# Linear attention in a decoder layer: paired feature tiles, 64-row fp32 scores by row halves, scores copied by ScalarE, later keys cleared by GpSimd, and GpSimd's sums behind the rows of norm 2

## The reference

```python
h = _ln(x, g1, beta1)
q = _phi((h @ wq).reshape(b, s, H, DH), proj)     # _phi(x) = elu(x @ proj) + 1
k = _phi((h @ wk).reshape(b, s, H, DH), proj)
v = (h @ wv).reshape(b, s, H, DH)
def step(carry, qkv_t):                            # scan over the tokens, so causal
    kv = kv + k_t[..., :, None] * v_t[..., None, :]
    ksum = ksum + k_t
    num = jnp.einsum('bhd,bhde->bhe', q_t, kv)
    den = jnp.einsum('bhd,bhd->bh', q_t, ksum) + 1e-06
    return ((kv, ksum), num / den[..., None])
x = x + attn.reshape(b, s, H * DH) @ wo
h2 = _ln(x, g2, beta2)
x = x + (gelu(h2 @ w1 + b1) @ w2 + b2)
```

## Time and profile before

| what | value |
|---|---|
| device time, median of 3 runs | 2541.67 us (2539.79 to 2542.41) |
| the profiled execution | 2538.4 us, of which the span from first to last instruction is 2536.7 us |
| mean granted TensorE clock | 0.949 of full speed |
| busy: PE, PEld | 2320.6 us (91%), 1752.5 us (69%) |
| busy: DVE, ACT, POOL | 1872.8 us (74%), 1573.8 us (62%), 678.4 us (27%) |

### The profile page before, as it was taken

How to read it: one execution, slowest core, us unless ns; L and a number is a source line. 1 busy time by engine, 2 the same in 40 slices (tenths; PEclk the granted TensorE clock), 3 DMA queues, 4 the chain that set the end, 5 groups by cost and what they waited for, 6 DMA issues and landing times. The chain is left out here.

```text
span 2536.7 us, 61265 instructions
## 1 busy us (share of the span) xinstructions
PE 2320.6 (91%) x20194; PEld 1752.5 (69%) x20194; DVE 1872.8 (74%) x4914; ACT 1573.8 (62%) x3456; POOL 678.4 (27%) x1179
## 2 busy tenths in 40 slices
PE   5998988988987589999999999999999999879997
PEld 3866856857757357676667767776767667667886
DVE  5667557657665478888888888888888888666657
ACT  4344244253351278888888888888888888544444
POOL 2001001001001234444444344444444444200003
PEclk8999999999999799999999999999999999758999
DMA  4100000000000200000000000000000000023302
GB/s 124 37 1 1 0 0 0 0 0 0 0 0 1 90 11 10 15 14 8 13 8 13 8 13 8 13 8 13 11 11 13 8 7 1 1 68 100 100 1 59
DMA packets 45652, 50.08 MB, mean 20 GB/s; under 512 B 19120, under 2 KB 37664, under 8 KB 45504
## 3 DMA queue, kind: packets, MB, share of 16 engines
q1 hardware_dynamic: 45504, 48.45, 6.6%
HBM read 44.78 MB, written 3.67 MB: 19 GB/s over the span
## 5 line engine op out<-in xcount | busy, mean ns | idle before, releaser
L1393 POOL TENSOR_SCALAR p_norm<-p,p_rec 112x375 f32<-112x375 f32 x512 | 305.1, 596 | 728.4 <-DVE p_rec L1235 674.7
L1117 ACT ACTIVATE p<-s_neg,neg_max 112x375 f32<-112x375 f32 x512 | 311.3, 608 | 131.6 <-DVE neg_max L1230 101.3
L1239 DVE TENSOR_TENSOR pt_lo<-b_t,pt_hi 125x336 f16<-125x336 f32 x512 | 259.5, 507 | 115.7 <-ACT pt_hi L1123 100.1
L1008 PE MATMUL b_t<-ident,p_norm 112*125 112x112 f32 x1536 | 287.7, 297 | 9.5 <-POOL p_norm L1393 8.9
L1215 DVE SCALAR_TENSOR_TENSOR k<-b_pb,k 64x375 f16<-64x375 f32 x512 | 280.9, 549 | 13.5 <-ACT k L1108 2.5
L1230 DVE CUSTOM_DVE_ANT_0 s_neg<-b_s,mask_bias 112x375 f32<-112x375 f32 x512 | 275.9, 539 | 0.8 <-PE b_s L1002 0.7
L1108 ACT ACTIVATE k<-b_pb 64x375 f16<-64x375 f32 x512 | 243.9, 476 | 26.7 <-PE b_pb L64 23.7
L1008 PEld LDWEIGHTS b_t<-ident,p_norm 112*125 112x125 f32 x1536 | 217.0, 193 | 54.3 <-POOL p_norm L1393 31.5
L1123 ACT ACTIVATE pt_hi<-b_t 125x336 f16<-125x336 f32 x512 | 226.5, 442 | 34.2 <-issue 16.1
L417 ACT ACTIVATE o_hi<-a_pb 128x448 f16<-128x448 f32 x64 | 34.9, 545 | 320.3 <-PE a_pb L309 320.1
L638 POOL TENSOR_SCALAR a_rstd<-a_mom 112x4 f32<-112x4 f32 x24 | 5.5, 230 | 769.3 <-DVE a_mom L470 769.3
(11 more groups left out here) (247 smaller groups left out, 6871.2 us busy)
## 6 DMA issues: line engine op xcount, KB each, us to landing
w_raw<-in_L_ffn_W_dram SPq DMA_DIRECT2D x16, 1024.0 KB, 7.5
ctx<-in_ctx_dram SPq DMA_DIRECT2D x32, 375.0 KB
out_dram<-c_z SPq DMA_DIRECT2D x8, 448.0 KB, 3.2
x_sb<-in_x_dram SPq DMA_DIRECT2D x1, 3136.0 KB, 19.4
ff<-in_L_attn_w_dram SPq DMA_DIRECT2D x2, 1024.0 KB, 7.0
b_stage<-in_L_xattn_Wkv_dram SPq DMA_DIRECT2D x2, 1024.0 KB, 10.3
mask<-in_mask_BxS_bf_dram SPq DMA_DIRECT2D x32, 41.0 KB, 2.6
a_raw<-in_L_attn_wq_dram SPq DMA_DIRECT2D x1, 1024.0 KB, 5.0
```

Of the source, the lines that this page charges most:

```text
L1008: mm = pe.transpose(t_ps[h % 2][0:JP, t * T:(t + 1) * T], p_norm[:, h % 4, t * JP:(t + 1) * JP], ident[0:T, 0:T])
L1117: act.activation(p32[:, h % 4, :], s_neg[:, h % 2, :], ACT.Exp, bias=neg_max[:, h % 4:h % 4 + 1], scale=-1.0, accum_out=p_sum[:, h % 4:h % ...
L1239: dve.tensor_tensor(pt_lo[:, h % 4, :], t_ps[h % 2][0:JP, 0:JT * T], pt_hi[:, h % 4, :], ALU.subtract).then_inc(pt_lo_done, 1)
L1393: pool.tensor_scalar(p_norm[:, h % 4, :], p32[:, h % 4, :], p_rec[:, h % 4:h % 4 + 1], 0.0, ALU.mult, ALU.add).then_inc(p_norm_done, 1)
```

## The change

The k features get paired tiles like q's: `kt` has 8 tiles of 128 partitions, written by one DVE instruction per tile; `kz` and its memset are gone. A score product reads 64 partitions of `kt` and `qt`: heads with even number the partitions 0 to 63, heads with odd number 64 to 127. Units are renumbered so that an even unit holds four even heads and the next one their four neighbours; `scores` is issued for two units at even steps, the two halves in turn, each half into its own PSUM bank. It waits for `s_copied` of both units before. ACT copies each unit's scores to `sm` (`take_scores`), which has four buffers where it had two, and POOL clears the later keys there in place with a select (`mask`). DVE's `mask` and the matrix `causal` are gone. `turn_output` is issued at odd steps with four transposes. POOL's two sums wait for `rows_done[1]` too, the rows of norm 2.

```diff
@@ -114,18 +113,18 @@
...
-        NSM = 2
+        NSM = 4
...
-        kz = sb("kz", [P, H, GT], F32)
+        kt = sb("kt", [P, KI, GT], F32)
...
-        o32 = sb("o32", [T, 4, 4 * DH], F32)
+        o32 = sb("o32", [T, 2, 8 * DH], F32)
...
@@ -146,6 +145,12 @@
+        def unit(u):
+            b, quad = divmod(u, 4)
+            first = 8 * (quad // 2) + quad % 2
+            return b, [first + 2 * i for i in range(4)]
...
@@ -164,7 +169,7 @@
...
-                if TURN_AT <= t < UNITS + TURN_AT and (t - TURN_AT) % 2 == 0:
+                if TURN_AT <= t < UNITS + TURN_AT and (t - TURN_AT) % 2 == 1:
...
@@ -284,31 +289,33 @@
...
-                b, quad = divmod(u, 4)
-                at_least(pe, s_masked, UNITS * g + u - 1)
-                for i in range(4):
-                    h = 4 * quad + i
-                    mm = pe.matmul(s_ps[u % 2][0:T, i * T:(i + 1) * T], kz[:, h, b * T:(b + 1) * T],
-                                   qt[:, h // 2, b * T:(b + 1) * T], start=True, stop=True)
-                mm.then_inc(s_ready, 1)
+                b, heads = unit(u)
+                cols = slice(b * T, (b + 1) * T)
+                at_least(pe, s_copied, UNITS * g + u)
+                for i, h in enumerate(heads):
+                    for r in range(2):
+                        rows = slice(DH * r, DH * (r + 1))
+                        mm = pe.matmul(s_ps[r][0:T, i * T:(i + 1) * T], kt[rows, h // 2, cols], qt[rows, h // 2, cols],
+                                       start=True, stop=True)
+                        if i == 3:
+                            mm.then_inc(s_ready, 1)
...
-                b, quad = divmod(u, 4)
+                b, heads = unit(u)
...
-                for i in range(4):
+                for i, h in enumerate(heads):
...
-                                   v1[0:T + 1, b, 4 * quad + i, :], start=True, stop=True)
+                                   v1[0:T + 1, b, h, :], start=True, stop=True)
...
-            def turn_output(g, u):
-                pe.wait_ge(o_done, UNITS * g + u + 1)
-                ps = claim(use(g, "O", u // 2)) if u % 2 == 0 else bank(use(g, "O", u // 2))
-                for m in range(2):
-                    c = (2 * (u % 2) + m) * T
-                    mm = pe.transpose(ps[:, c:c + T], o32[:, u % 4, m * P:(m + 1) * P], ident[0:T, 0:T])
-                if u % 2 == 1:
-                    mm.then_inc(pb_ready, 1)
+            def turn_output(g, j):
+                pe.wait_ge(o_done, UNITS * g + 2 * j + 2)
+                ps = claim(use(g, "O", j))
+                for m in range(4):
+                    mm = pe.transpose(ps[:, m * T:(m + 1) * T], o32[:, j % 2, m * P:(m + 1) * P], ident[0:T, 0:T])
+                mm.then_inc(pb_ready, 1)
...
@@ -320,12 +327,12 @@
...
-                    if t < UNITS:
+                    if t < UNITS and t % 2 == 0:
...
-                    if TURN_AT <= t < UNITS + TURN_AT:
-                        turn_output(g, t - TURN_AT)
+                    if TURN_AT <= t < UNITS + TURN_AT and (t - TURN_AT) % 2 == 1:
+                        turn_output(g, (t - TURN_AT) // 2)
...
@@ -417,12 +424,20 @@
...
+            def take_scores(g, u):
+                act.wait_ge(s_ready, UNITS * g + u - u % 2 + 2)
+                at_least(act, av_done, UNITS * g + u + 1 - NSM)
+                act.activation(sm[0:T, u % NSM, :], s_ps[u % 2][0:T, 0:4 * T], ACT.Identity).then_inc(s_copied, 1)
...
+                    if t < UNITS and t % 2 == 0:
+                        take_scores(g, t)
+                        take_scores(g, t + 1)
...
@@ -489,21 +504,9 @@
...
-                if kind == "K":
-                    for r in range(2):
-                        rows = slice(DH * r, DH * (r + 1))
-                        ins = dve.scalar_tensor_tensor(kz[rows, 2 * i + r, :], ps[rows, 0:GT], 0.0, phi_exp[rows, i % 2, :],
-                                                       ALU.max, ALU.add)
-                else:
-                    ins = dve.scalar_tensor_tensor(qt[:, i, :], ps[:, 0:GT], 0.0, phi_exp[:, i % 2, :], ALU.max, ALU.add)
-                ins.then_inc(free_of(u), 1)
-            def mask(g, u):
-                dve.wait_ge(s_ready, UNITS * g + u + 1)
-                at_least(dve, av_done, UNITS * g + u + 1 - NSM)
-                dve.tensor_tensor(sm[0:T, u % NSM, :].rearrange("p (i t) -> p i t", t=T),
-                                  s_ps[u % 2][0:T, 0:4 * T].rearrange("p (i t) -> p i t", t=T),
-                                  causal[:, :].unsqueeze(1).to_broadcast([T, 4, T]), ALU.mult).then_inc(s_masked, 1)
+                dst = kt if kind == "K" else qt
+                dve.scalar_tensor_tensor(dst[:, i, :], ps[:, 0:GT], 0.0, phi_exp[:, i % 2, :], ALU.max,
+                                         ALU.add).then_inc(free_of(u), 1)
...
@@ -514,7 +517,8 @@
...
-                dve.tensor_tensor(o32[:, u % 4, :].rearrange("p (i d) -> p i d", d=DH), ps[:, :, 0:DH],
+                dst = o32[:, u // 2 % 2, :].rearrange("p (i r d) -> p r i d", r=2, d=DH)[:, u % 2, :, :]
+                dve.tensor_tensor(dst, ps[:, :, 0:DH],
...
@@ -540,8 +544,6 @@
...
-                    if t < UNITS:
-                        mask(g, t)
...
@@ -616,7 +618,6 @@
...
-            dve.wait_ge(kz_zeroed, 1)
...
@@ -639,21 +640,28 @@
...
+            def mask(g, u):
+                settle(pool, passed, (s_copied, UNITS * g + u + 1))
+                rows = sm[0:T, u % NSM, :].rearrange("p (i t) -> p i t", t=T)
+                pool.affine_select(out=rows, in_=rows, compare_op=ALU.is_ge, fill=0.0, base=0, pattern=[[0, 4], [1, T]],
+                                   channel_multiplier=-1).then_inc(s_masked, 1)
...
+                    if t < UNITS:
+                        mask(g, t)
...
-                at_least(pool, rows_done[2], g)
+                settle(pool, passed, (rows_done[1], g + 1), (rows_done[2], g))
...
-            pool.memset(kz[:, :, :], 0.0).then_inc(kz_zeroed, 1)
...
@@ -699,17 +707,14 @@
...
-            pool.memset(causal[:, :], 1.0).then_inc(consts_done, 1)
...
-            pool.wait_ge(consts_done, 3)
+            pool.wait_ge(consts_done, 2)
...
-            pool.affine_select(out=causal[:, :], in_=causal[:, :], compare_op=ALU.is_ge, fill=0.0, base=0,
-                               pattern=[[1, T]], channel_multiplier=-1).then_inc(consts_done, 1)
...
-            pe.wait_ge(consts_done, 5)
+            pe.wait_ge(consts_done, 3)
...
```

More of the change, by code:

```diff
@@ L106, in layer1 @@
         b2 = sb("a_b2", [T, D], F32)
-        causal = sb("causal", [T, T], F32)
-        load_layer1(nc, a, x_sb, ident, half_neg, consts_done, causal, hi, lo, (g1, be1, g2, be2, b1, b2), sb_in, psum_in, sem)
+        load_layer1(nc, a, x_sb, ident, half_neg, consts_done, hi, lo, (g1, be1, g2, be2, b1, b2), sb_in, psum_in, sem)
         def pair(name, k, c0, n, width):
@@ L220, in layer1 @@
         h_hi_done = [sem(f"a_h_hi_done{i}") for i in range(2)]
-        kz_zeroed, pads_done = sem("a_kz_zeroed"), sem("a_pads_done")
+        pads_done = sem("a_pads_done")
         relu_done, exp_done = sem("a_relu_done"), sem("a_exp_done")
-        s_ready, s_masked, av_done, rec_done, o_done, o_hi_done = (
-            sem(f"a_{n}") for n in ("s_ready", "s_masked", "av_done", "rec_done", "o_done", "o_hi_done"))
+        s_ready, s_copied, s_masked, av_done, rec_done, o_done, o_hi_done = (
+            sem(f"a_{n}") for n in ("s_ready", "s_copied", "s_masked", "av_done", "rec_done", "o_done", "o_hi_done"))
         xs1_done, xs_done = sem("a_xs1_done"), sem("a_xs_done")
@@ L661, in _, with load_layer1 @@
             ln_rstd(NG - 1, 2)
-def load_layer1(nc, a, x_sb, ident, half_neg, consts_done, causal, hi, lo, vectors, sb_in, psum_in, sem):
+def load_layer1(nc, a, x_sb, ident, half_neg, consts_done, hi, lo, vectors, sb_in, psum_in, sem):
     stack = ExitStack()
```

## The result

The changed kernel takes 2421.74 us (median of 4 runs, 2419.57 to 2433.45) against 2540.73 us for the kernel before, run again beside it: ratio 0.9544, interval 0.9511 to 0.9577. The profiled execution has a span of 2420.4 us, 116.3 less than before.

A forecast was written before the change was run, and what follows sets the result against it. TensorE was taken to bound the attention and feed-forward stages, waits the projection stage. Terms 5.2 + 1.2 + 50.4 + 4.1 + 17.6 = 78.5 us off 2538.4 gave 2459.9, stated as 2462 us; range 2440 to 2514.

The forecast's parts named there:

- Sum: Whole kernel: start 5.2, prologue K tiles 1.2, projection stages 50.4, group 7's rows 4.1, attention stages 17.6; 78.5 us saved.
- Start: Kernel start: kz's memset goes, sm's doubles, PE starts 5.2 us earlier; prologue K tiles save another 1.2 us.
- Norm 2 and K tiles: Projection stage: first wait 3.9, clock 1.8, K tiles' pace 0.9, shorter kz wait 0.6; 7.2 us per group.
- Rival B: Projection stage gives back half as ACT's work comes to the front: 3.9 instead of 7.2 us, 2485 us; chance 0.09.
- Scores: Attention stage: row halves overlap, a pair takes 1.17 us with switches instead of 1.57; 3.2 us saved per group.
- Rival A: Attention-stage scores: row halves don't overlap, a pair costs 1.95 us, 50 us more than forecast, 2512 us; chance 0.20.
- Attention stage: Each of 8 groups: scores save 3.2 us, uncovered first copies cost 1.0; 2.2 us net, 17.6 in all.
- Last group: Group 7: norm 2's rows in front of T2 save 4.1 us; its attention stage saves 2.2.
- Select: POOL's masking select of 448 columns in the attention stage takes 0.7 us, covered in steady state.
- C: Attention stage: POOL's selects hold up DVE's line 477 rows through the port, 45 us, 2507 us; chance 0.06.
- D: Attention stage: POOL's select is slow, at 2.3 us it loses 98 us, 2560 us, slower than before; chance 0.04.
- the 0.31 us wait: Attention-stage group start: the only part of DVE's masks the prediction took to be on PE's path.

The follow-up runs named there:

- b_act100: Kernel before plus 100 empty ScalarE instructions at the start of layer 2, putting its loop where the changed kernel has it: 2507.33 us, ratio 0.9874.
- a_act156: Changed kernel plus 156 empty ScalarE instructions at layer 2's start, its loop back at the earlier place within 256 instructions: 2466.3 us, ratio 0.9728.
- b_wait: Kernel before with one line of the change, GpSimd's sums waiting for norm 2's rows: 2496.11 us, ratio 0.9842.
- a_serial: Changed kernel with a scores pair's products ordered half after half (rows 0 to 63, then 64 to 127) instead of alternating: 2543.5 us, ratio 1.0013.
- a_twice: Changed kernel with the eight products of each scores pair computed twice in a row, same output: 2492.97 us, ratio 0.9823.
- a_dvemask: Changed kernel with masks on VectorE as before, without ScalarE's copy and GpSimd's select: 2507.45 us, ratio 0.9875.
- a_act64: Changed kernel plus 64 empty ScalarE instructions at the start of layer 2: 2407.34 us, ratio 0.949.
- a_pool145: Changed kernel plus 145 empty GpSimd instructions at layer 2's start, its loop 256 instructions behind its earlier place: 2428.95 us in one run.
- a_dve118: Changed kernel plus 118 empty VectorE instructions at layer 2's start, its loop exactly where it was before the change: 2423.32 us in one run.

## Why the prediction missed

**The step that failed is the sum's scope.** "Sum: 5.2 + 1.2 + 50.4 + 4.1 + 17.6 = 78.5 us" counts the edited layer alone and gives all else nothing. The 100 instructions that copies and waits add to ScalarE's list moved its loop of layer 2 to a better place: 32.4 us where the sum has 0. This is shown by b_act100 (31.6 us less than the kernel before in its own runs, with no other edit) and a_act156. The profile of before had the row for it, 13 waits of ScalarE on "issue", and the sum had no bound for what would become of them. That they would go was luck: an edit of another length could have left them or brought more. Without this the time would have been about 2454 us (2421.7 + 32.4), inside the range.

**The terms of layer 1**, 84.8 for 78.5 (some 2 us of it only because the group that the sum went by, 98.38 us, is shorter than the mean of the others before, 98.7):

- Start: T1 at 33.30 us (33.2 forecast), first scores 7.1 us earlier (6.4). Right.
- Norm 2 and K tiles: 26.10 - 19.12 = 6.98 us per group (7.2). Right, as is its split: 5.75 (5.7) for wait and clock by b_wait, 1.23 (1.5) for the K tiles. PE's first wait, for `qt`, is 0.6 us and not below 0.5; that for `kt` is 1.0, the 1.62 less 0.6 that was forecast. Rival B is out.
- Scores: 0.61 us less for the pair and 0.22 more around it, 0.38 a step as forecast (0.40). Rival A is out, by the timeline after and by a_serial, which shows what it takes: neighbours in different halves. The Trainium skill, "TensorEngine Tiling (Array Packing)", section "Key Properties", says that tiles load weights and multiply in parallel and that a change of tiling mode drains TensorE. The trace agrees with the first: the halves work at once (49 ns a record). For the second it has a price, 0.41 us a pair for the way in and out (a_twice); what happens in that time it does not show.
- Attention stage: 42.69 - 39.11 = 3.58 us (2.2). This is the mis-sized term, + 1.4 us x 8 = 11 us. The scores of the first four units and the values of the first two take 253.06 - 248.15 = 4.91 us for 5.24 before, 0.3 less in spite of the 1.18 us wait, where by my terms they would take 1.0 - 0.8 = 0.2 more; the rest is spread over steps that were not of the steady 1.73 us before, and no run took it apart.
- Feed-forward stage: 29.86 us for 29.59 before, 0.27 longer in each group, where the sum has nothing. No run took it apart.
- Last group: 4.2 us for 4.1 + 2.2. In layer 2 ScalarE waits for its first weight's transfer before and after (28.7 and 30.2 us), which may take some of it back.
- Select: 0.58 us (0.7), VectorE 23.74 us busy in the stage, none of PE's waits on it: C and D are out. Of C's mechanism a little is seen: the eight rows of line 477 (492 after) that stand beside the selects take up to 515 ns, where 404 were the rule before. That the move is needed at all a_dvemask shows (4 us a group, and more with the clock); I had given it the 0.31 us wait only.

## What to carry to other kernels

An edit moves the code of everything behind it: before giving unchanged loops nothing, look in their waits for "issue", or for an engine that had long been done, once a round, and at the packets of the instruction queue, and give what you find a bound of both signs. Then a few empty instructions ahead of the loop are a cheap test, and here a gain of 25 us by themselves (a_act64). And where two halves of the array are to work at once, write their products in turn.

## What the hardware showed that I had not expected

- A loop of 319 records on ScalarE loads five packets of code in each round or none, by its place: 98 packets in the whole run or 33. An even batch takes 38.9 us with none, and 40.4 or 43.0 with five, by whether a border lies just behind the jump.
- A wait of 2.10 us on TensorE is followed by 3.4 us at granted clock 0.50 in the loop before; one of 0.65 us is not.
- 64-row products of one half keep the 98 ns a record of full units; only the other half's products beside them bring a pair down to 49. Issued half after half, a pair is 1.45 us, and the clock fell after a wait of 1.15 us in each group and stayed at 0.50 while TensorE was busy for 13.20 of 13.20 us; alternated, it stayed at 1.00 after 1.18 us.
- In group 0 the clock falls for 24 us in the profiles of a_act64 and a_pool145 and not in those of the changed kernel, a_act156 and a_dve118, with the same work there: 99.4 us for 88.3. What decides it stays open; no run took it apart.
